# Half of the bias moved from VectorE to GpSimd, the scale of the levels folded into a mask, and the output scale one step later, in a fused convolution and 8-bit dense kernel

## The chip, the cores and the metric

The kernel runs on one core of a Trainium2 chip. The metric is the device time of one execution in microseconds (us), here the median of three runs. Engines are named as in the profile: PE is TensorE (PEld its weight loads), DVE is VectorE, ACT is ScalarE, POOL is GpSimd, SP is SyncE, which only issues DMAs in this kernel.

## The reference, cut to what matters

```python
def fake_quant(x, bits, axis):
    bound = 2 ** (bits - 1) - 1
    scale = max(abs(x), axis) / bound           # 1 where it is 0
    return round(clip(x / scale, -bound, bound)) * scale

h = conv1d(x, weight, taps=9, padding=4, groups=4)       # x: 64 x 64 x 1024
h = h + (cond_128 @ c_weight.T)[:, :, None] + fside_S_0[None, :, None]
xq = fake_quant(h, 8, axis=-1)                  # one scale per row of 1024
kq = fake_quant(ffn_kernel, 8, axis=0)          # 1024 x 1024, one scale per column
y = xq @ kq + fake_quant(ffn_bias, 16, axis=-1)
return x + fake_quant(y, 8, axis=-1)            # again one scale per row
```

## The kernel before, in words

The 4096 rows of length 1024 are cut into 32 tiles (`TILES`) of 128 rows: 8 samples by the 16 channels of one group. All five engines run program text written out by hand; each has its own loop over steps k, and semaphores join them. Several tiles are in flight at once. The order of the work is this order of the text, engine by engine; nothing is planned by a scheduler.

What happens to tile t, with the functions that do it:

- SP loads the convolution windows (`load_xwin`), and later the plain rows of x for the final sum (`load_x`, into a ring `o_sb` of 5, which also holds the output until `store` sends it).
- ACT rounds the windows to `x_hi` (`round_x`, L265), POOL makes the rest `x_lo` (`split`, L218), and PE does the convolution as 14 matmuls of 512 columns (`conv`, L386 and L396).
- DVE takes a maximum per block of the convolution (`column_max`, L564) and multiplies it by a 0/1 mask into `col_max` (L572). PE spreads it over the rows (`spread_max`, L407). DVE then makes the row maximum (L579), the scale of the levels `scale8` = maximum/127, not under 2^-126 (L582), the row's scale `row_scale` (L585), the inverse (L590) and half of the 8-bit levels (L594): all in `levels`. ACT makes the other half (`round_levels`, L304).
- PE transposes the levels one step later (`turn_levels`, L416), ACT copies them to `a_t` (`take_levels`, L295), and PE multiplies them by the dense kernel in two halves of 512 columns, 8 matmuls each (`dense`, L427): half 0 in step t+2, half 1 in step t+4 (`LAG = (2, 4)`). Each half has one PSUM bank of `dense_ps`.
- DVE scales each half in place in PSUM (`scale_half`, L550) and adds the bias `bq`, writing to the SBUF ring `y` of 5 tiles (`add_bias`, L559). The next `dense` of that half waits for `biased0` or `biased1`.
- One step behind the second half, in step t+5 (`TAIL = 5`), DVE takes the maximum of the whole row of y and makes its scale and inverse (`out_scale`, L604, L608, L611), ACT rounds y to levels and scales them back (`quantise`, L312 and L315), POOL adds x (`add_x`, L227), and SP stores.
- The last tile's output is made in halves by ACT (`quantise_last`, L323) and DVE (`add_x_last`, L618), and stored in halves (`store_last`, L185).

A write to a slot of `y` waits until the tile that had it five tiles before has been added (`o_made`). In a step k of its loop, DVE does: `column_max(k)`, `out_scale(k-5)`, `scale_half(k-2, 0)`, `levels(k)`, `add_bias(k-2, 0)`, `scale_half(k-4, 1)`, `add_bias(k-4, 1)`. ACT does: `take_levels(k-1)`, `round_x(k+2)`, `quantise(k-5)`, `round_levels(k)`. POOL does: `split(k+2)`, `add_x(k-5)`. PE does: `conv(k)`, `turn_levels(k-1)`, `dense(k-2, 0)`, `spread_max(k)`, `dense(k-4, 1)`; in step 32 the last transpose, of tile 31, stands behind `dense(30, 0)` and `dense(28, 1)`.

## Time and profile before

| | |
|---|---|
| median of 3 runs | 280.97 us (279.19 to 281.17) |
| the profiled execution | 278.56 us |
| its span, first to last instruction | 276.7 us |
| PE busy | 251.1 us, 91% of the span |
| DVE busy | 238.8 us, 86% |
| ACT busy | 185.2 us, 67% |
| POOL busy | 153.8 us, 56% |
| mean granted clock of PE | 0.986 |
| chain that ended last | PE 81%, DVE 8%, ACT 4%, DMA 3%, issue 2% |

The span is the stretch of one profiled execution that the trace shows; 1.86 us of that execution lie outside it. Instructions of one engine can overlap a little in the trace, so the start of the next one often lies before the end that the row gives. "Idle before" and the name behind the arrow say how long the engine stood still before a row and whose work released it. The chain that ended last is followed back from the last instruction, and what it names is what set the end.

### The profile page before, as it was taken

How to read it: one execution, taken by the hardware profiler on the slowest of the kernel's cores; microseconds unless marked ns; L12 is line 12 of the kernel's file. 1: busy time of each engine (PE TensorE's matmuls, PEld its weight loads, DVE VectorE, ACT ScalarE, POOL GpSimd, SP SyncE). 2: the span in 40 equal slices, each digit the busy share in tenths (PEclk: the TensorE clock that was granted, in tenths of full speed). 3: DMA queues.
4: the chain of work that ended last, by engine and by line, in shares of the span. 5: the costliest groups of instructions: out<-in, count | busy, mean ns of one | idle time of the engine just before them, and what ended most of it. 6: DMA issues, size and time to landing. Idle time of an engine off the chain costs nothing.

```text
span 276.7 us, 4240 instructions
## 1 busy us (share of the span) xinstructions
PE 251.1 (91%) x1372; PEld 163.5 (59%) x1372; DVE 238.8 (86%) x509; ACT 185.2 (67%) x278; POOL 153.8 (56%) x71
## 2 busy tenths in 40 slices
PE   7866769999999999999999999999999999997540
PEld 3555557666666666666666666666666666663210
DVE  1799964799999999999999999999999989999984
ACT  6257586477777777777777777777777767564762
POOL 2533333356666666666666666666666666533453
PEclk9979999999999999999999999999999999999996
DMA  6997322406666565566666766666666663333355
GB/s 253 416 408 301 123 84 103 153 0 227 223 203 212 211 202 212 203 217 217 209 204 210 230 228 228 228 227 226 219 203 197 218 218 117 144 142 139 107 220 219
DMA packets 15799, 56.04 MB, mean 203 GB/s; under 512 B 1954, under 2 KB 1954, under 8 KB 15778
## 3 DMA queue, kind: packets, MB, share of 16 engines
q1 hardware_dynamic: 15488, 55.71, 56.8%
q8 instruction: 11, 0.18, 0.3%
q10 hardware_dynamic: 290, 0.07, 0.1%
q14 instruction: 10, 0.08, 0.1%
HBM read 38.99 MB, written 16.78 MB: 202 GB/s over the span
## 4 chain that ended last, share of the span: by engine, by line
PE 81%; DVE 8%; ACT 4%; DMA 3%; issue 2%; SPq 0%; DVEq 0%
PE dense_ps L427 36%; PE conv_ps L396 31%; PE turn_ps L416 5%; PE conv_ps L386 5%; DMA k_raw<-ffn_kernel 3%; DVE dense_ps L550 2%; DVE y L559 2%; DVE y_max L604 2%; ACT kq L279 2%; PE small_ps L407 2%; PE dense_ps L449 1%; DVE k_max L523 1%; ACT a_int L304 1%; PE dense_ps L440 1%; ACT x_hi L265 1%
## 5 line engine op out<-in xcount | busy, mean ns | idle before, releaser
L427 PE MATMUL dense_ps<-kq,a_t 128*128 128x512 bf16 x512 | 120.6, 379 | 6.1 <-DVE y L559 5.0
L218 POOL TENSOR_TENSOR x_lo<-xwin,x_hi 128x1032 fp32r<-128x1032 f32 x32 | 76.6, 2393 | 80.8 <-ACT x_hi L265 80.8
L227 POOL TENSOR_TENSOR o_sb<-y,o_sb 128x1024 f32<-128x1024 f32 x31 | 73.9, 2384 | 32.8 <-ACT y L315 32.7
L427 PEld LDWEIGHTS dense_ps<-kq,a_t 128*128 128x128 bf16 x512 | 48.9, 101 | 53.7 <-issue 6.7
L295 ACT CAST a_t<-turn_ps 128x1024 bf16<-128x1024 int16 x32 | 32.4, 1012 | 48.5 <-PE turn_ps L416 48.5
L564 DVE TENSOR_REDUCE small_ps<-conv_ps 128x8 f32<-128x1024 f32 x32 | 39.4, 1232 | 13.8 <-PE conv_ps L396 13.5
L550 DVE SCALAR_TENSOR_TENSOR dense_ps<-dense_ps,row_scale,k_scale_b 128x512 f32<-128x512 f32 x64 | 47.7, 745 | 3.6 <-PE dense_ps L427 3.6
L312 ACT ACTIVATE y_int<-y,y_inv 128x1024 int16<-128x1024 f32 x31 | 35.6, 1148 | 22.3 <-DVE y_inv L611 22.1
L559 DVE TENSOR_TENSOR y<-dense_ps,bq 128x512 f32<-128x512 f32 x64 | 43.9, 685 | 2.8 <-ACT bq L288 1.6
L604 DVE TENSOR_REDUCE y_max<-y 128x1 f32<-128x1024 f32 x32 | 38.7, 1210 | 0.7 <-issue 0.2
L304 ACT ACTIVATE a_int<-conv_ps,inv 128x128 int16<-128x128 f32 x128 | 36.0, 363 | 1.1 <-DVE inv L590 1.1
L315 ACT ACTIVATE y<-y_int,y_scale 128x1024 f32<-128x1024 int16 x31 | 35.7, 1153 | 1.0
L396 PE MATMUL conv_ps<-x_hi,w_hi 128*128 128x512 f32 x128 | 36.2, 405 | 0.0
L265 ACT CAST x_hi<-xwin 128x1032 fp32r<-128x1032 f32 x32 | 33.8, 1055 | 3.0 <-DMA xwin<-x_windows 3.0
L396 PE MATMUL conv_ps<-x_hi,w_lo 128*128 128x512 f32 x128 | 35.5, 399 | 0.0
L396 PE MATMUL conv_ps<-x_lo,w_hi 128*128 128x512 f32 x128 | 35.2, 397 | 0.0
L396 PEld LDWEIGHTS conv_ps<-x_hi,w_lo 128*128 128x128 f32 x128 | 24.4, 191 | 6.2
L396 PEld LDWEIGHTS conv_ps<-x_lo,w_hi 128*128 128x128 f32 x128 | 24.0, 188 | 6.2 <-POOL x_lo L218 0.2
L396 PEld LDWEIGHTS conv_ps<-x_hi,w_hi 128*128 128x128 f32 x128 | 24.7, 193 | 4.8
L386 PE MATMUL conv_ps<-select,ctx 128*128 128x512 f32 x64 | 25.0, 474 | 1.9 <-ACT x_hi L265 1.6
L594 DVE TENSOR_TENSOR a_int<-conv_ps,inv 128x512 int16<-128x512 f32 x32 | 22.1, 691 | 1.1
L416 PE MATMUL turn_ps<-ident_b,a_int 128*128 128x128 bf16 x256 | 19.8, 220 | 1.6 <-ACT a_int L304 1.6
(55 smaller groups left out, 160.2 us busy)
## 6 DMA issues: line engine op xcount, KB each, us to landing
xwin<-x_windows SPq DMA_DIRECT2D x32, 516.0 KB, 4.8
o_sb<-x_rows SPq DMA_DIRECT2D x32, 512.0 KB, 5.3
out<-o_sb SPq DMA_DIRECT2D x31, 512.0 KB, 2.9
k_raw<-ffn_kernel SPq DMA_DIRECT2D x4, 1024.0 KB, 10.5
w_raw<-taps SPq DMA_DIRECT2D x2, 256.0 KB, 3.2
b_row<-ffn_bias SPq DMA_DIRECT2D x1, 512.0 KB, 15.9
out<-o_sb SPq DMA_DIRECT2D x2, 256.0 KB, 2.7
condt<-cond_t ACTq DMA_DIRECT2D x1, 32.0 KB
```

Source lines behind the costliest of these rows:

```text
L218: pool.tensor_tensor(x_lo[:, at].rearrange("p n b -> p (n b)"), xwin[:, t % XWIN, :], x_hi[:, at].bitcast(F32).rearrange("p n b -> p (n b) ...
L227: pool.tensor_tensor(o_sb[:, at, :], y[:, t % YRING, :], o_sb[:, at, :], ALU.add).then_inc(s["o_made"], 1)
L265: act.copy(x_hi[:, t % XSPLIT].rearrange("p n b -> p (n b)"), xwin[:, t % XWIN, :]).then_inc(s["hi_made"], 1)
L304: ins = act.activation(a_int[:, at, n * BLOCKS:(n + 1) * BLOCKS], conv_cols(at)[:, n, :], ACT.Copy, scale=inv8[:, at, n:n + 1])
L315: act.activation(y[:, t % YRING, :], y_int[:, t % 2], ACT.Copy, scale=y_scale[:, t % 2:t % 2 + 1]).then_inc(s["y_dequantised"], 1)
L386: mm = pe.matmul(conv_ps[:, at, hs, :].rearrange("p (n b) -> p n b", n=NH), ctx2[:, g].rearrange("k q o -> k (q o)"), select[:, ns].unsque ...
L396: mm = pe.matmul(conv_ps[:, at, hs, :].rearrange("p (n b) -> p n b", n=NH), w[:, ch, g].rearrange("p q o -> p (q o)"), x[:, x_at, hs * NH: ...
L427: mm = pe.matmul(dense_ps[:, h, :], a_t[:, t % LEVELS, q].rearrange("b j o -> b (j o)"), kq[:, q, half(h)], start=(q == 0), stop=(q == Q - 1))
L550: dve.scalar_tensor_tensor(out=dense_ps[:, h, :], in0=dense_ps[:, h, :], scalar=row_scale[:, t % RSRING:t % RSRING + 1], in1=k_scale_b[:, ...
L559: dve.tensor_tensor(y[:, t % YRING, half(h)], dense_ps[:, h, :], bq[:, half(h)], ALU.add).then_inc(s[f"biased{h}"], 1)
L564: dve.tensor_reduce(cmax_ps, conv_ps[:, t % 2].rearrange("p h (n b) -> p (h n) b", b=BLOCKS), AX_X, ALU.max, apply_absolute_value=True).th ...
L604: dve.tensor_reduce(y_max[:, at], y[:, t % YRING, :], AX_X, ALU.max, apply_absolute_value=True).then_inc(s["y_max_made"], 1)
```

## The change

Four things are changed:

1. The bias of half 1 is no longer added by DVE in the step from PSUM to SBUF. DVE's `scale_half(t, 1)` writes its product to `y` in SBUF, and POOL adds `bq` in place there (a new `add_bias` of POOL, one step later, in step t+5, at the head of POOL's step). For the last tile, 31, DVE does both halves as before. Half 0 is as before.
2. `dense(t, 1)` on PE waits for `scaled1` in place of `biased1`.
3. The factor 1/127 and the floor are put into the step that masks the column maximum (`mask_q` = mask/127, a scalar_tensor_tensor with maximum and multiply), so what is spread is already the scale. The operation that made `scale8` (L582) is gone; the inverse is taken from the row maximum itself. `mask_q` is made once at the start.
4. `TAIL` is 6, not 5: `out_scale`, `quantise`, `add_x`, the load of x for it and the store of a tile all stand one step later in their engines' loops.

```diff
-TAIL = LAG[1] + 1
+TAIL = LAG[1] + 2
...
+        def pool_adds(t, h):
+            return h == 1 and t < LAST
...
+            def add_bias(t, h):
+                wait(pool, f"scaled{h}", t + 1)
+                wait(pool, "b_made", 1)
+                pool.tensor_tensor(y[:, t % YRING, half(h)], y[:, t % YRING, half(h)],
+                                   bq[:, half(h)], ALU.add).then_inc(s[f"biased{h}"], 1)
...
             for k in range(TILES + TAIL):
+                if there(k - LAG[1] - 1) and pool_adds(k - LAG[1] - 1, 1):
+                    add_bias(k - LAG[1] - 1, 1)
                 if there(k + 2):
                     split(k + 2)
                 if 0 <= k - TAIL < LAST:
...
             def dense(t, h):
                 wait(pe, "a_made", t + 1)
-                wait(pe, f"biased{h}", t)
+                wait(pe, "scaled1" if h else "biased0", t)
...
             def scale_half(t, h):
                 wait(dve, f"dense_made{h}", t + 1)
-                dve.scalar_tensor_tensor(out=dense_ps[:, h, :], in0=dense_ps[:, h, :],
+                if pool_adds(t, h):
+                    wait(dve, "o_made", t - YRING + 1)
+                    to = y[:, t % YRING, half(h)]
+                else:
+                    to = dense_ps[:, h, :]
+                dve.scalar_tensor_tensor(out=to, in0=dense_ps[:, h, :],
...
-                dve.tensor_tensor(col_max[:, t % 2], cmax_ps.unsqueeze(2).to_broadcast([P, NS, Q]),
-                                  mask[:].unsqueeze(1).to_broadcast([P, NS, Q]), ALU.mult
-                                  ).then_inc(s["col_max_masked"], 1)
+                dve.scalar_tensor_tensor(out=col_max[:, t % 2],
+                                         in0=cmax_ps.unsqueeze(2).to_broadcast([P, NS, Q]),
+                                         scalar=127 * TINY,
+                                         in1=mask_q[:].unsqueeze(1).to_broadcast([P, NS, Q]),
+                                         op0=ALU.max, op1=ALU.mult
+                                         ).then_inc(s["col_max_masked"], 1)
...
-                dve.tensor_scalar(scale8[:, at], rmax_ps, 1.0 / 127, TINY, ALU.mult,
-                                  ALU.max).then_inc(s["scale_made"], 1)
+                dve.reciprocal(inv8[:, at], rmax_ps).then_inc(s["inv_made"], 1)
...
-                wait(dve, "scale_made", t + 1)
-                dve.reciprocal(inv8[:, at], scale8[:, at]).then_inc(s["inv_made"], 1)
...
                 wait(dve, "biased0", t + 1)
-                wait(dve, "biased1", t + 1)
+                if pool_adds(t, 1):
+                    wait(dve, "biased1", t + 1)
+                else:
+                    wait(dve, "biased_last", 1)
...
                     scale_half(k - LAG[1], 1)
-                    add_bias(k - LAG[1], 1)
+                    if not pool_adds(k - LAG[1], 1):
+                        add_bias(k - LAG[1], 1)
```

POOL's queue at the end of the program, before: the last `split`, then one `add_x` after another, of the tiles 24 to 30 (the number in `x_in` is the tile's, modulo 5).

```order
L218 TENSOR_TENSOR x_lo<-xwin,x_hi 128x1032 [waits conv_made,hi_made]
L227 TENSOR_TENSOR o_sb<-y,o_sb 128x1024 [waits x_in4,y_dequantised]
L227 TENSOR_TENSOR o_sb<-y,o_sb 128x1024 [waits x_in0,y_dequantised]
L227 TENSOR_TENSOR o_sb<-y,o_sb 128x1024 [waits x_in1,y_dequantised]
L227 TENSOR_TENSOR o_sb<-y,o_sb 128x1024 [waits x_in2,y_dequantised]
L227 TENSOR_TENSOR o_sb<-y,o_sb 128x1024 [waits x_in3,y_dequantised]
L227 TENSOR_TENSOR o_sb<-y,o_sb 128x1024 [waits x_in4,y_dequantised]
L227 TENSOR_TENSOR o_sb<-y,o_sb 128x1024 [waits x_in0,y_dequantised]
```

And now, from the `add_x` of tile 25 on. The rows that write `y` are the new `add_bias`, here of the tiles 27 to 30; the one of tile 28 stands behind the `add_x` of tile 26, the one of tile 30 behind that of tile 28.

```order
L236 TENSOR_TENSOR o_sb<-y,o_sb 128x1024 [waits x_in0,y_dequantised]
L229 TENSOR_TENSOR y<-y,bq 128x512 [waits b_made,scaled1]
L236 TENSOR_TENSOR o_sb<-y,o_sb 128x1024 [waits x_in1,y_dequantised]
L229 TENSOR_TENSOR y<-y,bq 128x512 [waits b_made,scaled1]
L236 TENSOR_TENSOR o_sb<-y,o_sb 128x1024 [waits x_in2,y_dequantised]
L229 TENSOR_TENSOR y<-y,bq 128x512 [waits b_made,scaled1]
L236 TENSOR_TENSOR o_sb<-y,o_sb 128x1024 [waits x_in3,y_dequantised]
L229 TENSOR_TENSOR y<-y,bq 128x512 [waits b_made,scaled1]
L236 TENSOR_TENSOR o_sb<-y,o_sb 128x1024 [waits x_in4,y_dequantised]
L236 TENSOR_TENSOR o_sb<-y,o_sb 128x1024 [waits x_in0,y_dequantised]
```

DVE's queue at the end, before: the output scale of tile 30 (L604, L608, L611), the second half of tile 31 (L550, L559), and the output scale of tile 31.

```order
L604 TENSOR_REDUCE y_max<-y 128x1 [waits biased1,biased0]
L608 TENSOR_SCALAR y_scale<-y_max 128x1 [waits y_dequantised,y_max_made]
L611 RECIPROCAL y_inv<-y_scale 128x1 [waits y_scale_made]
L550 SCALAR_TENSOR_TENSOR dense_ps<-dense_ps,row_scale,k_scale_b 128x512 [waits dense_made1]
L559 TENSOR_TENSOR y<-dense_ps,bq 128x512 [waits o_made,b_made,scaled1]
L604 TENSOR_REDUCE y_max<-y 128x1 [waits biased1,biased0]
L608 TENSOR_SCALAR y_scale<-y_max 128x1 [waits y_dequantised,y_max_made]
L611 RECIPROCAL y_inv<-y_scale 128x1 [waits y_scale_made]
```

And now: the second half of tile 31 stands ahead of the output scale of tile 30, and the two output scales follow one another (L569 is `scale_half`, L578 `add_bias`, L626, L630 and L633 are `out_scale`).

```order
L569 SCALAR_TENSOR_TENSOR dense_ps<-dense_ps,row_scale,k_scale_b 128x512 [waits dense_made1]
L578 TENSOR_TENSOR y<-dense_ps,bq 128x512 [waits o_made,b_made,scaled1]
L626 TENSOR_REDUCE y_max<-y 128x1 [waits biased1,biased0]
L630 TENSOR_SCALAR y_scale<-y_max 128x1 [waits y_dequantised,y_max_made]
L633 RECIPROCAL y_inv<-y_scale 128x1 [waits y_scale_made]
L626 TENSOR_REDUCE y_max<-y 128x1 [waits biased_last,biased0]
L630 TENSOR_SCALAR y_scale<-y_max 128x1 [waits y_dequantised,y_max_made]
L633 RECIPROCAL y_inv<-y_scale 128x1 [waits y_scale_made]
```

`out_scale(30)` waits for POOL's `biased1` there, and `out_scale(31)` is behind it.

## Rows read from the trace of the kernel before

**Rows 1.** Windows: one period of the main loop (busy us and instructions of each engine).

```profile
core 0: us, PE busy (x) PEld busy (x) DVE busy (x) ACT busy (x) POOL busy (x), PEclk, DMA share, GB/s
143.43:150.76 7.33, 7.33 (x41) 4.83 (x41) 6.73 (x15) 5.29 (x8) 4.76 (x3) 1.00 0.63 217
```

**Rows 2.** Chain that ended last, in order of time: start us, us, what.

```profile
48.20 0.46 PE turn_ps L416 x8
48.66 1.73 PE dense_ps L427 x8
...
52.72 2.82 PE conv_ps L396 x12
55.54 0.46 PE turn_ps L416 x8
...
246.31 1.24 DVE small_ps L564
```

**Rows 3.** Groups by line and shape: xcount | busy us, mean ns | idle before, releaser.

```profile
L227 POOL TENSOR_TENSOR o_sb<-y,o_sb 128x1024 f32<-128x1024 f32 x31 | 73.9, 2384 | 32.8 <-ACT y L315 32.7
...
L550 DVE SCALAR_TENSOR_TENSOR dense_ps<-dense_ps,row_scale,k_scale_b 128x512 f32<-128x512 f32 x64 | 47.7, 745 | 3.6 <-PE dense_ps L427 3.6
L559 DVE TENSOR_TENSOR y<-dense_ps,bq 128x512 f32<-128x512 f32 x64 | 43.9, 685 | 2.8 <-ACT bq L288 1.6
...
L315 ACT ACTIVATE y<-y_int,y_scale 128x1024 f32<-128x1024 int16 x31 | 35.7, 1153 | 1.0
L312 ACT ACTIVATE y_int<-y,y_inv 128x1024 int16<-128x1024 f32 x31 | 35.6, 1148 | 22.3 <-DVE y_inv L611 22.1
...
L572 DVE TENSOR_TENSOR col_max<-small_ps,mask 128x64 f32<-128x64 f32 x32 | 7.2, 224 | 1.1
...
L582 DVE TENSOR_SCALAR scale<-small_ps 128x8 f32<-128x8 f32 x32 | 5.3, 166 | 1.1
...
L210 POOL TENSOR_TENSOR w_lo<-w_raw,w_hi 128x512 fp32r<-128x512 f32 x2 | 2.7, 1352 | 4.3 <-ACT w_hi L258 4.3
```

**Rows 4.** Timeline, one step of the main loop: start us, us, engine, line [idle before].

```profile
144.90 0.22 DVE L572 TENSOR_TENSOR col_max<-small_ps,mask 128x64 f32<-128x64 f32 x1
...
145.40 0.41 PEld L407 LDWEIGHTS small_ps<-col_max,same_b 128*128 128x128 f32 x2
...
146.13 2.38 POOL L218 TENSOR_TENSOR x_lo<-xwin,x_hi 128x1032 fp32r<-128x1032 f32 x1 [2.02 <-ACT x_hi L265]
```

**Rows 5.** Timeline, behind the last convolution (tail).

```profile
256.10 1.01 ACT L295 CAST a_t<-turn_ps 128x1024 bf16<-128x1024 int16 x1 [3.39 <-PE turn_ps L416]
...
257.01 1.15 ACT L312 ACTIVATE y_int<-y,y_inv 128x1024 int16<-128x1024 f32 x1
...
258.19 1.15 ACT L315 ACTIVATE y<-y_int,y_scale 128x1024 f32<-128x1024 int16 x1
...
259.42 4.81 POOL L227 TENSOR_TENSOR o_sb<-y,o_sb 128x1024 f32<-128x1024 f32 x2 [5.30 <-ACT y L315]
...
262.42 1.22 DVE L604 TENSOR_REDUCE y_max<-y 128x1 f32<-128x1024 f32 x1
...
262.47 1.89 PE L427 MATMUL dense_ps<-kq,a_t 128*128 128x512 bf16 x8 [1.67 <-DVE y L559]
...
264.06 1.15 ACT L312 ACTIVATE y_int<-y,y_inv 128x1024 int16<-128x1024 f32 x1 [2.26 <-DVE y_inv L611]
```

**Rows 6.** Timeline, the end, and the one line L618.

```profile
270.02 2.35 POOL L227 TENSOR_TENSOR o_sb<-y,o_sb 128x1024 f32<-128x1024 f32 x1 [1.20 <-ACT y L315]
...
271.17 1.33 ACT L323 ACTIVATE y_int<-y,y_inv 128x512 int16<-128x512 f32 x2 [1.22 <-DVE y_inv L611]
...
272.39 0.33 SPq L180 DMA_DIRECT2D out<-o_sb  x1
...
273.61 0.36 SPq L185 DMA_DIRECT2D out<-o_sb  x1
...
L618 DVE SCALAR_TENSOR_TENSOR o_sb<-y_int,y_scale,o_sb x2: 739/831/923, 272.0 to 272.8; 128x512 f32<-128x512 int16 x2
```

More of the change, by code:

```diff
@@ L54, in build @@
         mask = sb("mask", [P, NS], F32)
+        mask_q = sb("mask_q", [P, NS], F32)
         same = sb("same", [P, CG], F32)
@@ L83, in build @@
         col_max = sb("col_max", [P, 2, NS, Q], F32)
-        scale8 = sb("scale8", [P, 2, NS], F32)
         inv8 = sb("inv8", [P, 2, NS], F32)
@@ L106, in build @@
             "cond_in", "b_in", "ones_made", "ident_made", "ident_b_made", "warm_made",
-            "mask_made", "same_made", "same_b_made", "select_made", "cond_made", "ctx_mm",
+            "mask_made", "mask_q_made", "same_made", "same_b_made", "select_made", "cond_made", "ctx_mm",
             "ctx_rounded", "ctx_made", "w_hi_made", "w_lo_made",
@@ L112, in build @@
             "hi_made", "lo_made", "conv_made", "col_max_made", "col_max_masked",
-            "max_spread", "row_max_made", "scale_made", "picked_made", "inv_made", "a_rounded", "a_rounded_dve", "a_turned",
-            "a_made", "dense_made0", "dense_made1", "scaled0", "scaled1", "biased0", "biased1",
+            "max_spread", "row_max_made", "picked_made", "inv_made", "a_rounded", "a_rounded_dve", "a_turned",
+            "a_made", "dense_made0", "dense_made1", "scaled0", "scaled1", "biased0", "biased1", "biased_last",
             "y_max_made", "y_scale_made", "y_inv_made", "y_rounded", "y_dequantised", "o_made", "last_rounded", "last_made")}
@@ L502, in _ @@
                               ).then_inc(s["same_made"], 1)
+            dve.wait_ge(s["mask_made"], 1)
+            dve.tensor_scalar(mask_q[:], mask[:], 1.0 / 127, None, ALU.mult
+                              ).then_inc(s["mask_q_made"], 1)
             dve.wait_ge(s["same_made"], 1)
@@ L559, in add_bias @@
                 dve.tensor_tensor(y[:, t % YRING, half(h)], dense_ps[:, h, :], bq[:, half(h)],
-                                  ALU.add).then_inc(s[f"biased{h}"], 1)
+                                  ALU.add).then_inc(s["biased_last" if h else "biased0"], 1)
             def column_max(t):
@@ L570, in column_max @@
                 if t == 0:
-                    dve.wait_ge(s["mask_made"], 1)
-                dve.tensor_tensor(col_max[:, t % 2], cmax_ps.unsqueeze(2).to_broadcast([P, NS, Q]),
-                                  mask[:].unsqueeze(1).to_broadcast([P, NS, Q]), ALU.mult
-                                  ).then_inc(s["col_max_masked"], 1)
+                    dve.wait_ge(s["mask_q_made"], 1)
+                dve.scalar_tensor_tensor(out=col_max[:, t % 2],
[4 more added lines that the diff above has]
+                                         ).then_inc(s["col_max_masked"], 1)
             def levels(t):
@@ L581, in levels @@
                 wait(dve, "row_max_made", t + 1)
-                dve.tensor_scalar(scale8[:, at], rmax_ps, 1.0 / 127, TINY, ALU.mult,
-                                  ALU.max).then_inc(s["scale_made"], 1)
+                dve.reciprocal(inv8[:, at], rmax_ps).then_inc(s["inv_made"], 1)
                 wait(dve, "scaled1", t - RSRING + 1)
                 dve.tensor_tensor_reduce(out=picked[:, at], in0=rmax_ps, in1=mask[:],
-                                         scale=1.0 / 127, scalar=0.0, op0=ALU.mult, op1=ALU.add,
+                                         scale=1.0, scalar=0.0, op0=ALU.mult, op1=ALU.add,
                                          accum_out=row_scale[:, r_at:r_at + 1]
                                          ).then_inc(s["picked_made"], 1)
-                wait(dve, "scale_made", t + 1)
-                dve.reciprocal(inv8[:, at], scale8[:, at]).then_inc(s["inv_made"], 1)
                 wait(dve, "inv_made", t + 1)
```

## Prediction

> **What bounds the kernel now.** I read the chain in order of time first, then one period by windows, then the timeline behind the last convolution.
>
> In the chain the first and the last step of a period of the main loop are transposes on PE, at 48.20 and 55.54 [rows 2]. What lies between is PE alone: transposes, dense matmuls, the convolution. It stays so until 246.31, where a DVE row takes the chain over [rows 2]. The window of one period shows PE busy 7.33 of 7.33 us at a granted clock of 1.00, DVE only 6.73, ACT 5.29, POOL 4.76 [rows 1]. So some 198 us (246.31 - 48.20, 27 periods) are PE's own pace, and an engine that gets lighter there gives nothing. What the change can move is the tail, 246.31 to 276.7, some 30 us in which no convolution is left and DVE, ACT and POOL finish the last tiles one behind the other.
>
> **The change part by part.**
>
> *Main loop, DVE.* Gone: one bias add of 685 ns and one L582 of 166 ns per step [rows 3]. DVE's load falls from 6.73 to about 5.9 us of 7.33. Cover was complete before, so this gives 0.
>
> *Main loop, the masked maximum.* It becomes a two-operation form. The trace has no such row at 64 elements. Bounds: 224 ns as now [rows 3], and 284 ns, since at 512 elements the two-operation form takes 745 against 685 ns [rows 3]; I take 0.25. It ends at 144.90 + 0.22 = 145.12 and PE's load that wants it stands at 145.40 [rows 4]. That is 0.28 us of cover against at most 0.06 lost: 0. Without the cover it would be 32 x 0.06 = 1.9 us. Starting the inverse without L582 brings `levels` forward by 0.17 us, hidden too. The one `mask_q` at the start stands long before the first convolution's maximum: 0.
>
> *Main loop, POOL.* Added: one add of 128x512 per step. No row shows it. From below, half of the 2384 ns for 1024 columns, 1.19; from above the strided 128x512 row, 1.35 [rows 3]. I take 1.24, nearer to the first, since both operands are contiguous there and here. POOL idles 2.02 us ahead of `x_lo` [rows 4] and the add is ready to go in just that gap (`scaled1` of the step before is older), so `x_lo` is not even late. POOL's load becomes 4.76 + 1.24 = 6.0 of 7.33. The sum is 0. With `TAIL` at 6, SP's loads and stores and ACT's rounding move by one step together and keep their distances; a write to `y` waits for an `add_x` one period nearer, with some 4 us still in hand in the loop.
>
> *Main loop, the SBUF port.* The rows show DVE's `scale_half` at 745 ns over all 64 instructions, whatever POOL did beside it [rows 3]. The Trainium skill (SBUF — State Buffer, Who interferes with whom) says that a DVE instruction with two SBUF inputs and a GpSimd instruction that reads SBUF shut each other out. By that rule nothing changes in the loop, since each of these DVE operations has its other input in PSUM.
>
> *The tail.* Here the order counts. POOL's queue now alternates: add of tile 27, `add_x(26)`, add of tile 28, `add_x(27)`, and so on. I follow it with the durations of the rows.
> - ACT takes the last levels at 256.10 to 257.11 [rows 5]. DVE's saved 0.17 us pulls this to 256.94 at best. In both kernels one `quantise` stands right behind: before that of tile 27, now that of tile 26. So one more tile than before is still to do.
> - `quantise(26)`: 2.33 us (257.01 to 259.34 [rows 5]), so 256.84 to 259.17. `add_x(26)`, 2.38 us and 0.08 later: 259.25 to 261.63. Only then the add of tile 28: 261.66 to 262.9. Its second half had been scaled by DVE some 6 us before.
> - `out_scale(28)` on DVE. From the start of L604 to ACT's start it takes 1.64 us (262.42 to 264.06 [rows 5]). DVE is just then busy with the first half of tile 31, which waits for `add_x(26)` because it has its slot of `y`, and with `scale_half(29, 1)` (0.69 + 0.75 from 261.7). So 263.2 to 264.8.
> - `quantise(28)` 264.8 to 267.15; `add_x(28)` 267.2 to 269.6; then, behind it, the add of tile 30: 269.6 to 270.85.
> - `out_scale(30)` 270.95 to 272.6. `quantise(30)` 272.6 to 274.9. Meanwhile `out_scale(31)` is done by 274.2, so the last rounding starts behind `quantise(30)` at 274.9, where before it started at 271.17 [rows 6].
> - `add_x(30)` 275.0 to 277.4, and the store of tile 30 is issued at 277.4. Before it was issued at 272.39, at once after the `add_x` that began at 270.02 [rows 6], and the span ended 276.7 - 272.39 = 4.3 us later, with 1 MB of stores in that time. The halves of the last tile are ready at 276.6 and 277.3 and queue behind that store on SP. So 277.4 + 4.3 = 281.7.
>
> The sum: 0 in the loop, 0 at the start (the chain is DMA, ACT and PE there, none of the edited lines), +5.0 in the tail. Against the profiled execution 278.56 + 5.0 = 283.6. That execution lies 2.4 us under the median of the runs shown, 280.97; on that median it is 286.0, which I give. Bounds of the sum: the new add at 1.19 or 1.35, twice on the chain, is -0.1 to +0.2; if the stores overlap fully, -0.4; the handoffs between engines that I took as 0.03 to 0.1 us are ten or so, +-0.5. That is +4.2 to +5.7, plus the runs' own scatter of about 1 us to either side.
>
> *The very end.* L618 took 923 ns the first time, while POOL was in `add_x(30)` until 272.37, and 739 ns the second time, with POOL idle [rows 6]. Now both fall wholly into `add_x(30)`. If the slowing stays at some 0.18 us each, they end at 277.6 and change nothing. The section of the Trainium skill named above lets the second comer wait for the whole of the first's instruction, since L618 reads `y_int` and `o_sb`, both in SBUF. By that, L618 would end at 277.4 + 1.5 = 278.9 and the span at 278.9 + 3.1 = 282.0, from the last store's 273.61 to 276.7 [rows 6]. The row bears it out only in part: 0.38 us of overlap cost 0.18.
>
> **The rivals.**
>
> *Not slower: DVE's queue decides the tail, not POOL's.* In the tail of before DVE sets most of the chain. If POOL kept pace, DVE would pay one more `out_scale`, +1.64, and save four bias adds of 685 ns and the 0.17: -2.9. That makes 281.0 - 1.3 = 279.7. It decides if the adds of tiles 28 and 30 find POOL free. Against it: the order has each of them behind an `add_x` that waits for ACT, and rows 5 put the first of these past 259.3. Chance 0.12, for a tail that overlaps better than I see, down to a small loss.
>
> *Faster: the main loop is DVE's after all.* Then 0.85 us x 27 = 23 us would go, to 258. Against it stands PE's 7.33 of 7.33 [rows 1]. A few tenths per step, through a handoff that the rows hide, are all I can imagine: 276. Chance 0.04.
>
> *Slower by more: the loop loses its cover.* If POOL's add took over 2.0 us, or the masked maximum over 0.5, each step would pay. 0.1 us a step is 3 us: 289. Nothing in rows 1 or 4 speaks for it. Chance 0.04.
>
> *Slower by more: PE's clock falls in the tail.* PE now stands still from about 260.6 to 263.2, where before a gap of 1.67 us was followed by 8 matmuls in 1.89 us [rows 5], so full speed. At the lower of the two levels `dense(30, 1)` and `dense(31, 1)` take some 3.8 us each. Then tile 31's half is ready only at 273.1 and holds `out_scale(30)` behind it, 2.2 us late: 288.2. Chance 0.08.
>
> **How the numbers follow.** The forecast has 0.72: 286.0, its own range 284.5 to 287.5. Its lower edge, the not-slower rival and the clock case give a range of 282.5 to 288.5 for 8 in 10. A measurement of this kernel tells about 1% (2.8 us) from no change. Slower by over 1%: 0.72 + 0.04 + 0.08, less 0.04 for a forecast that comes out short: 0.80. Within 1%: 0.12 + 0.04 = 0.16. Faster: 0.04.
>
> **What would show it.** In the changed trace the period should still be 7.33 us with PE full, DVE near 5.9 and POOL near 6.0. In the tail, the add of tile 28 should start the moment `add_x(26)` ends, near 261.7, and the add of tile 30 right behind `add_x(28)`, near 269.6; the chain there should run POOL, DVE, ACT, POOL, with POOL's share no longer nil. The last rounding should start near 274.9 and the last stores be issued near 278. I am wrong if POOL idles ahead of the adds of tiles 28 and 30, if the period differs from 7.33, or if the last rounding starts before 273.

## The result, and the profile after

The changed kernel takes 286.84 us (median of 4 runs, 286.26 to 287.83) against 280.08 us for the kernel before on the same chip. The ratio is 1.0244, with a 95% interval of 1.0185 to 1.0302: slower, though whether by less or more than 2% stays open. The medians are 6.8 us apart. The profiled execution took 286.26 us with a span of 284.5 us, 7.8 us more than the 276.7 us before.

Where the 7.8 us are is read from the starts of the column maximum (L564 before, L583 after) of three tiles. This is the one row that marks each step of the main loop.

| stretch | before | after | more |
|---|---|---|---|
| start to column maximum of tile 4 | 48.24 | 51.00 | +2.8 |
| from there to that of tile 31 | 198.07 | 198.30 | +0.2 |
| from there to the end (the tail) | 30.4 | 35.2 | +4.8 |

First, the main loop of the kernel after, one period by windows (to be laid beside [rows 1]), and the tail as one window:

```profile
core 0: us, PE busy (x) PEld busy (x) DVE busy (x) ACT busy (x) POOL busy (x), PEclk, DMA share, GB/s
146.28:153.63 7.35, 7.35 (x41) 4.83 (x41) 5.88 (x13) 5.30 (x8) 6.02 (x4) 1.00 0.65 216
249.30:284.50 35.20, 15.51 (x82) 6.91 (x79) 23.97 (x42) 17.84 (x20) 20.63 (x12) 0.86 0.50 180
```

PE is still busy in all of the period, 7.35 of 7.35 us. DVE has fallen from 6.73 to 5.88 us and POOL has risen from 4.76 to 6.02, each as worked out, and next to nothing of it shows in the time (+0.2 us over 27 periods). In the tail PE has nothing like a full load.

Whoever reads only the chain that ended last is led astray here. Part 4 of the page after says:

```profile
POOL 46%; issue 44%; DVE 3%; DMA 3%; ACT 1%; ACTq 0%; SPq 0%; POOLq 0%; DVEq 0%; PE 0%
```

The chain now runs through POOL and "issue" for most of the main loop, although the window above has PE full and the period is that of before. I read it as one way back among several that end close together. For what bounds the loop, the window and the period decide, and not the share.

Groups by line and shape, after; they answer to [rows 3]:

```profile
L229 POOL TENSOR_TENSOR y<-y,bq 128x512 f32<-128x512 f32 x31 | 39.3, 1267 | 1.0 <-DVE y L569 1.0
...
L569 DVE SCALAR_TENSOR_TENSOR y<-dense_ps,row_scale,k_scale_b 128x512 f32<-128x512 f32 x31 | 23.0, 743 | 0.8 <-POOL o_sb L236 0.6 <-PE dense_ps L438 0.2
...
L591 DVE SCALAR_TENSOR_TENSOR col_max<-small_ps,mask_q 128x64 f32<-128x64 f32 x32 | 7.2, 225 | 1.1
...
L604 DVE RECIPROCAL inv<-small_ps 128x8 f32<-128x8 f32 x32 | 6.7, 208 | 1.1
```

POOL's new add takes 1.267 us (1.24 taken, bounds 1.19 and 1.35). DVE's product into SBUF takes 743 ns, as into PSUM. The masked maximum with its second operation takes 225 ns where it was 224 [rows 3]. So the fusion of the scale costs nothing per instruction, and L582's 166 ns are gone.

The tail of the kernel after, timeline (to be laid beside [rows 5] and [rows 6]):

```profile
259.81 1.15 ACT L323 ACTIVATE y_int<-y,y_inv 128x1024 int16<-128x1024 f32 x1
...
262.22 2.35 POOL L236 TENSOR_TENSOR o_sb<-y,o_sb 128x1024 f32<-128x1024 f32 x1 [3.89 <-ACT y L326]
...
264.53 1.26 POOL L229 TENSOR_TENSOR y<-y,bq 128x512 f32<-128x512 f32 x1
...
264.70 0.69 DVE L578 TENSOR_TENSOR y<-dense_ps,bq 128x512 f32<-128x512 f32 x1 [2.03 <-POOL o_sb L236]
...
265.96 1.21 DVE L626 TENSOR_REDUCE y_max<-y 128x1 f32<-128x1024 f32 x1
...
266.19 1.89 PE L438 MATMUL dense_ps<-kq,a_t 128*128 128x512 bf16 x8 [2.60 <-DVE y L569]
...
272.31 1.26 POOL L229 TENSOR_TENSOR y<-y,bq 128x512 f32<-128x512 f32 x1
...
273.67 1.22 DVE L626 TENSOR_REDUCE y_max<-y 128x1 f32<-128x1024 f32 x1 [1.25 <-POOL y L229]
...
277.55 1.32 ACT L334 ACTIVATE y_int<-y,y_inv 128x512 int16<-128x512 f32 x2
277.72 2.34 POOL L236 TENSOR_TENSOR o_sb<-y,o_sb 128x1024 f32<-128x1024 f32 x1 [1.84 <-ACT y L326]
```

The add of tile 28 (264.53) follows `add_x(26)` (262.22) at once. DVE's L578, the first half of tile 31, has stood 2.03 us until that same `add_x(26)` was done. The output scale of tile 30 (273.67) stood 1.25 us for POOL's add of tile 30. The last rounding starts at 277.55.

### The profile page after: what moved, and what is told of

Same layout as the page of the kernel before. It is cut to its first block, busy times and chain, and to the rows that moved or that the text cites. A ratio compares the mean times of both kernels' runs of the same rounds, so it can differ in the third digit from the quotient of the medians.

```text
span 284.5 us, 4235 instructions
## 1 busy us (share of the span) xinstructions
PE 253.6 (89%) x1372; PEld 164.3 (58%) x1372; DVE 213.7 (75%) x447; ACT 185.0 (65%) x278; POOL 191.7 (67%) x102
## 4 chain that ended last, share of the span: by engine, by line
POOL 46%; issue 44%; DVE 3%; DMA 3%; ACT 1%; ACTq 0%; SPq 0%; POOLq 0%; DVEq 0%; PE 0%
POOL x_lo L221 26%; POOL y L229 14%; POOL o_sb L236 6%; DMA k_raw<-ffn_kernel 3%; DVE k_max L537 1%; DVE o_sb L640 1%; ACT kq L290 1%; ACTq L41 0%; DVE y_max L626 0%; ACT y_int L323 0%; ACT x_hi L276 0%; SPq L163 0%; DVE k_int L548 0%; DVEq L41 0%; PE dense_ps L460 0%
## 5 line engine op out<-in xcount | busy, mean ns | idle before, releaser
L438 PE MATMUL dense_ps<-kq,a_t 128*128 128x512 bf16 x512 | 122.3, 383 | 6.1 <-DVE y L569 3.5
L583 DVE TENSOR_REDUCE small_ps<-conv_ps 128x8 f32<-128x1024 f32 x32 | 39.4, 1232 | 41.2 <-PE conv_ps L407 41.2
L323 ACT ACTIVATE y_int<-y,y_inv 128x1024 int16<-128x1024 f32 x31 | 35.6, 1148 | 24.4 <-DVE y_inv L633 24.4
L626 DVE TENSOR_REDUCE y_max<-y 128x1 f32<-128x1024 f32 x32 | 38.7, 1210 | 2.0 <-POOL y L229 1.8
L229 POOL TENSOR_TENSOR y<-y,bq 128x512 f32<-128x512 f32 x31 | 39.3, 1267 | 1.0 <-DVE y L569 1.0
L407 PE MATMUL conv_ps<-x_hi,w_lo 128*128 128x512 f32 x128 | 36.2, 405 | 0.0
L276 ACT CAST x_hi<-xwin 128x1032 fp32r<-128x1032 f32 x32 | 33.8, 1056 | 3.2 <-DMA xwin<-x_windows 3.2
L569 DVE SCALAR_TENSOR_TENSOR dense_ps<-dense_ps,row_scale,k_scale_b 128x512 f32<-128x512 f32 x33 | 24.5, 743 | 6.4 <-PE dense_ps L438 6.4
L578 DVE TENSOR_TENSOR y<-dense_ps,bq 128x512 f32<-128x512 f32 x33 | 22.5, 682 | 3.9 <-POOL o_sb L236 2.0
L569 DVE SCALAR_TENSOR_TENSOR y<-dense_ps,row_scale,k_scale_b 128x512 f32<-128x512 f32 x31 | 23.0, 743 | 0.8 <-POOL o_sb L236 0.6
```

Source lines behind the costliest of these rows:

```text
L229: pool.tensor_tensor(y[:, t % YRING, half(h)], y[:, t % YRING, half(h)], bq[:, half(h)], ALU.add).then_inc(s[f"biased{h}"], 1)
L276: act.copy(x_hi[:, t % XSPLIT].rearrange("p n b -> p (n b)"), xwin[:, t % XWIN, :]).then_inc(s["hi_made"], 1)
L323: act.activation(y_int[:, t % 2], y[:, t % YRING, :], ACT.Copy, scale=y_inv[:, t % 2:t % 2 + 1]).then_inc(s["y_rounded"], 1)
L407: mm = pe.matmul(conv_ps[:, at, hs, :].rearrange("p (n b) -> p n b", n=NH), w[:, ch, g].rearrange("p q o -> p (q o)"), x[:, x_at, hs * NH: ...
L438: mm = pe.matmul(dense_ps[:, h, :], a_t[:, t % LEVELS, q].rearrange("b j o -> b (j o)"), kq[:, q, half(h)], start=(q == 0), stop=(q == Q - 1))
L569: dve.scalar_tensor_tensor(out=to, in0=dense_ps[:, h, :], scalar=row_scale[:, t % RSRING:t % RSRING + 1], in1=k_scale_b[:, half(h)], op0=A ...
```

## The experiments

Twelve runs, in the order in which they were made. "Tail" is from the start of the column maximum of tile 31 to the end of the span; before it is 30.4 us, after 35.2.

**1. The later step alone.** On the kernel before:

```diff
-TAIL = LAG[1] + 1
+TAIL = LAG[1] + 2
```

> The kernel before with TAIL = 6 and nothing else; VectorE still adds both biases. Theory 1 (the prediction's: the tail grows because GpSimd's adds of tiles 28 and 30 stand behind an add_x): here there are no such adds, so only one more output scale is left, about +1.6 us over before, a tail (from the last column maximum to the end) of about 32 us against 30.4. Theory 2 (the later step alone does it: one more quantise stands behind the last take_levels, the y slot of tile 31 is freed late, and the last rounding queues behind quantise(30)): the first half of tile 31 waits for add_x(26) until about 261.8 (times of the profile of before), the last rounding starts near 275.2 in place of 271.2, and the tail is 35 to 36 us, so +4.5 to +5.5 us. Theory 3, beside both: some 2 us of the changed kernel's loss are stretches at the lower TensorE clock in the start-up, and differ from run to run; then the runs of this kernel, whose start is that of before, show granted clocks between 0.96 and 0.99 too.

Measured: 288.77 us, ratio 1.0301 (1.0233 to 1.0368), tail 37.9 us. That is slower than the whole change. Theory 1's tail of 32 us is far off. Theory 2 holds in kind: the later step makes the tail grow by all that the change does, and more, without any add on POOL. Its size was too low, 37.9 us against a forecast of 35 to 36. Its tail has the row that matters, DVE's wait for the slot of `y`, and one that I had only as a rival, TensorE's clock:

```profile
265.13 0.69 DVE L559 TENSOR_TENSOR y<-dense_ps,bq 128x512 f32<-128x512 f32 x1 [2.04 <-POOL o_sb L227]
...
267.36 2.70 PE L427 MATMUL dense_ps<-kq,a_t 128*128 128x512 bf16 x8 [3.34 <-DVE y L559]
...
271.73 3.55 PE L427 MATMUL dense_ps<-kq,a_t 128*128 128x512 bf16 x8 [1.67 <-DVE y L559]
```

PE stands 3.34 us behind the waiting DVE. Of the two runs of 8 matmuls that follow the first takes 2.70 and the second 3.55 us, where 1.89 is normal [rows 5], so the lower of the two levels of the clock is on for the second. DVE waits for both. Together they are 2.5 us over the normal; 37.9 less that is 35.4 us, an estimate that is inside theory 2's range.

**2. VectorE adds in the tail.** The changed kernel, with VectorE's own bias add from tile 27 on:

```diff
         def pool_adds(t, h):
-            return h == 1 and t < LAST
+            return h == 1 and t < 27
...
                 wait(pe, "scaled1" if h else "biased0", t)
+                if h and t > 27:
+                    wait(pe, "biased_last", t - 27)
```

> The changed kernel, but VectorE adds the second half's bias from tile 27 on, as it did in the kernel before; GpSimd adds it for tiles 0 to 26 only, so no add stands behind an add_x in the tail. Theory 1: the tail comes back to about 32 us, some 3 us under the changed kernel. Theory 2: the tail stays at 34.5 to 36 us, within 1 us of the changed kernel and of the kernel with the later step alone.

Measured: 289.6 us, ratio 1.034 (1.0286 to 1.0395), tail 37.7 us. With no add behind an `add_x` in POOL's queue its tail is 2.5 us longer than that of the changed kernel, where theory 1 had it some 3 us shorter. Theory 1, the one of the prediction, falls here. Theory 2 had the tail within 1 us of both other kernels: it is so for experiment 1 and not for the changed one. Most of the 2.5 us is the clock again: the two runs of 8 matmuls take 2.53 and 3.57 us. PE stands 3.33 us ahead of them, for DVE's add of the bias; in the changed kernel it may use the bank once the half is scaled and stands 2.60 us, and the matmuls behind it are at full speed. That the shorter wait is what kept the clock up there is not shown.

**3. The add on POOL without the later step.** The changed kernel with `TAIL = LAG[1] + 1`.

> The changed kernel with TAIL back at 5. Theory A (a ring of waits): GpSimd's add, the output scale, the two quantise operations, add_x and the next add then follow one another in each period, 1.27 + 0.08 + 1.63 + 2.33 + 0.08 + 2.39 + 0.03 = 7.8 us against TensorE's 7.34, so the period becomes about 7.8 us and the time grows by about 0.46 x 27 = 12 us over the changed kernel's loop, less the 3 to 5 us that the shorter tail gives back: 292 to 297 us. Theory B (VectorE's 1.3 us of slack per period takes up the wait): the period stays 7.34 us and the tail is shorter, about 281 to 284 us.

Measured: 305.3 us, ratio 1.0897 (1.084 to 1.0954). The period is 7.75 us (windows; PE is busy 7.49 of it), so theory A. One of its steps:

```profile
252.79 1.27 POOL L229 TENSOR_TENSOR y<-y,bq 128x512 f32<-128x512 f32 x1
...
254.16 1.22 DVE L626 TENSOR_REDUCE y_max<-y 128x1 f32<-128x1024 f32 x1 [1.38 <-POOL y L229]
...
258.23 2.37 POOL L236 TENSOR_TENSOR o_sb<-y,o_sb 128x1024 f32<-128x1024 f32 x1 [4.16 <-ACT y L326]
...
260.55 1.27 POOL L229 TENSOR_TENSOR y<-y,bq 128x512 f32<-128x512 f32 x1
```

From one POOL add (252.79) to the next (260.55) it is 7.76 us, and the output scale waits 1.38 us for the add. The range of 292 to 297 was too low. The loop is 9.1 us longer than that of the changed kernel (207.4 against 198.3), less than the 12 expected. The tail is what I had wrong: I had let it get shorter, but the ring goes on in it, one tile per 7.7 us until the end, and it is 44.6 us. So in this kernel the add on POOL costs the loop its pace without the later step; the two parts of the change can't be judged apart.

**4. The last sum with one input in PSUM.** On the changed kernel:

```diff
-                    act.activation(y_int[:, at, half(h)], y[:, LAST % YRING, half(h)], ACT.Copy,
+                    act.activation(conv_ps[:, h, 0, :].bitcast(I32), y[:, LAST % YRING, half(h)], ACT.Copy,
...
-                    dve.scalar_tensor_tensor(out=o_sb[:, o_at, half(h)], in0=y_int[:, at, half(h)],
+                    dve.scalar_tensor_tensor(out=o_sb[:, o_at, half(h)], in0=conv_ps[:, h, 0, :].bitcast(I32),
```

> The changed kernel, but ScalarE writes the last tile's levels as int32 to two PSUM banks that are free by then, so VectorE's last two operations (L618 before, L640 after) have one input in SBUF and one in PSUM, and still overlap GpSimd's last add_x. Theory A (the two engines shut each other out of SBUF reads): the first of the two falls from 2.25 us to about 0.75 to 0.9, and is done before add_x(30); the last stores are then issued right behind that of tile 30, and the end comes 0.3 to 0.9 us earlier. Theory B (it was slow for another reason, the queue or the write to o_sb): it still takes over 2 us and the end stays.

Measured: 286.7 us, tail 35.3 us. The line of the changed kernel, and the same line here:

```profile
L640 DVE SCALAR_TENSOR_TENSOR o_sb<-y_int,y_scale,o_sb x2: 741/1496/2252, 278.4 to 280.5; 128x512 f32<-128x512 int16 x2
```

```profile
L642 DVE SCALAR_TENSOR_TENSOR o_sb<-conv_ps,y_scale,o_sb x2: 743/748/753, 278.7 to 279.4; 128x512 f32<-128x512 int32 x2
```

With both inputs in SBUF the first of the two takes 2252 ns and ends only behind `add_x(30)`; with one in PSUM (and as int32 in place of int16) they take 743 and 753 ns, beside the same `add_x(30)`. So theory A for the instruction. For the time it is worth nothing, and the 0.3 to 0.9 us expected did not come: from the start of `add_x(30)` to the end it is 6.8 us with it (277.72 to 284.5) and 6.9 without (278.14 to 285.0), since the store of tile 30 is issued only when that `add_x` is done, and all the last stores go with it.

**5 to 7. The start.** Five is the kernel before once more. Six and seven are the kernel before and the changed kernel with five idle fp32 matmuls of 512 columns, in three of TensorE's waits of the start-up:

```diff
+                if k == 1:
+                    keep_busy(conv_ps[:, 1, 0, :], 2)
                 if there(k):
                     conv(k)
...
                     spread_max(k)
+                    keep_busy(turn_bank, 1)
                     turn_levels(k - 1)
...
-                    k_turns(7, 8)
+                    k_turn(7)
+                    pe.wait_ge(s["a_made"], 2)
+                    keep_busy(turn_bank, 2)
+                    k_turn(8)
```

> The kernel before, unchanged, profiled once more. Theory L (the start-up part of the changed kernel's loss, 2.8 us in its profile, is a matter of when the lower TensorE clock falls in an execution, and the first profile of before was one with little of it): this profile shows two stretches at the lower clock in the first 50 us as the changed kernel's does, with the column maximum of tile 4 near 51 us in place of 48.2, and a span of 279 to 280 us. Theory C (the change brings them): the column maximum of tile 4 is near 48.2 us again, the clock near 0.986, the span 276.5 to 277.5 us.

Measured: 280.89 us (278.83 to 281.99), ratio 0.9999; column maximum of tile 4 at 48.98, clock 0.987. The profile alone spoke for theory C. The runs' clocks don't. Of 29 executions of the kernel before that were listed beside these kernels, 17 have a mean granted clock of 0.972 to 0.974 and take 281.3 to 282.4 us; 10 have 0.986 to 0.990 and take 277.9 to 279.5 us; two lie between. So before itself has two levels, some 2.8 us apart, and both of its profiles are of the quicker sort. All four runs of the changed kernel have 0.962 to 0.965.

The profiles of experiments 1 and 8 show it directly. Both are the kernel before with `TAIL` at 6, and experiment 8 with a larger ring of `y` (below); nothing else in the text of their start is changed. Their windows of the start, 14 to 24 and 40 to 48 us, first experiment 1, then 8 (the granted clock stands behind POOL):

```profile
14.00:24.00 10.00, 7.81 (x40) 5.93 (x36) 8.40 (x13) 5.48 (x6) 4.77 (x2) 0.66 0.98 402
40.00:48.00 8.00, 5.79 (x40) 3.41 (x38) 3.47 (x10) 4.44 (x9) 0.75 (x1) 0.79 0.38 133
```

```profile
14.00:24.00 10.00, 7.26 (x44) 5.55 (x42) 9.35 (x15) 6.34 (x7) 4.77 (x2) 0.83 0.95 387
40.00:48.00 8.00, 6.37 (x46) 4.94 (x46) 4.39 (x11) 6.07 (x12) 1.50 (x1) 1.00 0.38 133
```

The column maximum of tile 4 starts at 51.45 us in the first and at 48.91 in the second.

> The kernel before with five idle matmuls of 512 columns more on TensorE, in its three longest waits of the start-up (ahead of conv(1), ahead of the first turn_levels, between k_turn(7) and k_turn(8)). Under theory L these waits are what the clock falls after: with them filled the column maximum of tile 4 comes at 47 to 48.5 us in every execution, and the times lie at 277 to 279 us, closer together than the 279 to 282 us of before. Under theory C, or if the filling costs as much as it saves, the time stays at 279 to 281 us.

Measured: 279.02 us (277.9 to 279.49), ratio 0.992 (0.9879 to 0.9961): faster than before. All eight runs take what the quicker sort of before takes, so the slower sort is gone. The column maximum of tile 4 is at 48.65, just past the 47 to 48.5 expected.

> The changed kernel with the same five idle matmuls. What is left between it and the kernel before with them is the change without the start-up's clock: the prediction's tail term, +4.5 to +5.5 us. So near 283 us if the start-up is then free of the lower clock, and still near 287 us if the start-up's loss has another cause.

Measured: 284.07 us (283.26 to 285.41), ratio 1.0117 (1.0079 to 1.0156), tail 35.3 us. The windows of the start, 14 to 24 and 40 to 48 us, for before, after, and after with the waits filled:

```profile
14.00:24.00 10.00, 7.33 (x40) 5.83 (x41) 9.44 (x15) 6.43 (x7) 4.77 (x2) 0.83 0.97 380
40.00:48.00 8.00, 7.04 (x48) 5.31 (x48) 3.72 (x10) 5.41 (x10) 2.17 (x1) 1.00 0.39 135
```

```profile
14.00:24.00 10.00, 7.38 (x33) 5.60 (x32) 8.28 (x13) 5.55 (x7) 4.77 (x2) 0.66 0.99 397
40.00:48.00 8.00, 5.94 (x37) 3.68 (x38) 3.89 (x10) 4.44 (x9) 0.32 (x1) 0.79 0.37 133
```

```profile
14.00:24.00 10.00, 8.18 (x50) 5.48 (x47) 9.79 (x14) 6.52 (x7) 4.78 (x2) 1.00 0.99 395
40.00:48.00 8.00, 7.54 (x52) 5.48 (x52) 3.37 (x9) 5.21 (x9) 2.36 (x1) 1.00 0.37 135
```

The column behind POOL is the granted clock: 0.83 and 1.00, then 0.66 and 0.79, then 1.00 and 1.00. A mean of 0.66 over 10 us is 6.8 us at 1.2 GHz, a mean of 0.79 over 8 us is 3.4 us. In the second stretch the run of 8 dense matmuls (at 42.53 after, 41.42 before) takes 3.55 us in the changed kernel's profile in place of 1.89. With the starts filled in both, what is left between the two kernels is 284.07 - 279.02 = 5.05 us: the change itself, and close to the prediction's +5.0. It is not free of the clock altogether: three of the ten runs of experiment 7 still have 0.966 to 0.974. By the two profiles it is 4.5 us of span, +4.9 in the tail, +0.2 in the loop and -0.6 in the start.

**8. The ring of y.** The kernel of experiment 1 (the later step alone) with `YRING` 6 in place of 5.

> The kernel with the later step alone (TAIL = 6, VectorE adds both biases), with the ring of y at 6 tiles in place of 5. The tail of that kernel showed VectorE standing 2.04 us before the first half of tile 31, for add_x(26), and TensorE 3.3 us behind it, after which its clock fell. Theory R (the slot of y is what the later step costs): the wait is gone, TensorE does not stand so long, and the time falls from 288.8 us by 3 to 5 us, to 284 to 286 us. Theory O (one more output scale and quantise are the cost, the wait is hidden behind them): it falls by less than 1.5 us.

Measured: 284.81 us (282.07 to 286.2), ratio 1.0116 (1.0069 to 1.0163), tail 33.8 us against 37.9. Theory R: one slot more takes 4 us away. Two things are gone in this profile, the wait of 2.04 us for the slot and the lower clock in the tail, which had cost the two runs of 8 matmuls 2.5 us; PE stands half as long ahead of the first of them:

```profile
263.15 1.89 PE L427 MATMUL dense_ps<-kq,a_t 128*128 128x512 bf16 x8 [1.67 <-DVE y L559]
...
266.70 1.89 PE L427 MATMUL dense_ps<-kq,a_t 128*128 128x512 bf16 x8 [1.67 <-DVE y L559]
```

How the 4 us divide between the two is not shown. The runs have two sorts of clock here as well.

**9 and 10. A tail put together from this.** `TAIL` is 5 again and VectorE adds the second half's bias. The scale stays folded into the mask. POOL adds half 0 of the last three tiles, and the last second halves get banks and an order of their own (ten is nine with the idle matmuls):

```diff
         def pool_adds(t, h):
-            return h == 1 and t < LAST
+            return h == 0 and t >= TILES - 3
...
-                    mm = pe.matmul(dense_ps[:, h, :],
+                    mm = pe.matmul(conv_ps[:, 0, t % 2, :] if late_bank(t, h) else dense_ps[:, h, :],
...
                     turn_levels(k - 1)
+                    if k == TILES:
+                        dense(k - LAG[1] + 1, 1)
...
+                if k == TILES + 1:
+                    scale_half(k - LAG[1], 1)
+                    add_bias(k - LAG[1], 1)
+                    scale_half(k - LAG[0], 0)
+                    continue
```

> The kernel before (TAIL = 5, VectorE adds the second half's bias) with what the earlier runs say of the tail: the scale folded into the mask; GpSimd adds the bias of half 0 for tiles 29, 30 and 31, whose sums are wanted some 10 us later; dense(29, 1) stands ahead of dense(31, 0) on TensorE, the second halves of tiles 30 and 31 go to two banks of conv_ps that are free by then, and VectorE takes scale_half(29, 1) ahead of scale_half(31, 0). If VectorE's queue sets the tail of before, three bias adds (2.1 us) and the waits for the bank (about 1 us) go: the tail falls from 30.4 to 27 to 28.5 us and the time by 2 to 3.5 us, to a ratio of 0.988 to 0.993. If ScalarE and GpSimd's chain behind the last take_levels sets it too, it falls by under 1 us.

Measured: 279.1 us (276.69 to 280.44), ratio 0.9955 (0.9906 to 1.0004), tail 28.2 us. The tail fell by 2.2 us as expected. The time did not show it beyond its interval, and the ratio missed the 0.988 to 0.993 expected: this profile has a slow stretch in the start (column maximum of tile 4 at 50.79), and the start's clock scatters by more than the gain.

> The kernel with the rearranged tail and the five idle matmuls in the start-up. The two gains stand in different places and should add up: the filled start-up gave a ratio of 0.992 by itself, so 0.980 to 0.985, about 276 us, and a spread of under 2 us between the runs. If the tail's gain depends on the clock, less.

Measured: 276.82 us (276.57 to 277.13), ratio 0.9889 (0.9833 to 0.9946), tail 28.2 us. This beats both kernels: 2.6 us under the median of before beside it (279.45), 10 us under the changed one. The time is close to the 276 expected, and the gain over experiment 6 is 2.2 us, at the low end of 2 to 3.5. The ratio missed the expected 0.980 to 0.985, since the kernel before had a median of 279.45 beside this one and of 281.38 beside experiment 6. `dense(29, 1)` and `dense(31, 0)` still start only at 256.65, behind 1.37 us of waiting for DVE's bias of tile 28.

**11 and 12. Which queue in the changed kernel?** Both have the start filled. POOL does its adds ahead in the tail, and twelve has `YRING` 6 besides:

```diff
-                if there(k - LAG[1] - 1) and pool_adds(k - LAG[1] - 1, 1):
-                    add_bias(k - LAG[1] - 1, 1)
+                for t in range(k - LAG[1] - (k <= TILES), k - LAG[1] + (k >= TILES)):
+                    if there(t) and pool_adds(t, 1):
+                        add_bias(t, 1)
```

> The changed kernel with the start-up filled (284.07 us), and in the tail GpSimd does its adds ahead: tiles 27 and 28 before add_x(26), 29 before add_x(27), 30 before add_x(28). Theory Q (the prediction's: GpSimd's alternating queue is what sets the tail): the add of tile 28 ends near 256 us in place of 262, the add of tile 30 no longer holds out_scale(30), and the time falls by 3 us or more. Theory S (the slot of y: VectorE stands before the first half of tile 31 until add_x(26) is done, so out_scale(28) comes no earlier whatever GpSimd does): only the waits of out_scale(29) and out_scale(30) for the adds go, 0.56 and 1.25 us in the changed kernel's profile, and the time falls by 1 to 1.5 us.

Measured: 283.64 us (282.06 to 285.19), ratio 1.0107 (1.0067 to 1.0147), tail 35.6 us, against 284.07 for experiment 7. POOL's add of tile 28 now starts at 256.68 in place of behind `add_x(26)`. Theory Q falls, since the time does not drop by 3 us and DVE's wait for the slot is as long as before. The medians are only 0.4 us apart, short of theory S's 1 to 1.5, but the clocks differ: four runs here and six of experiment 7 have 0.983 or more, and their medians are 282.6 and 283.8 us, the 1.2 us of theory S. In this profile the low clock in the tail takes the gain back. Its rows:

```profile
256.68 1.27 POOL L229 TENSOR_TENSOR y<-y,bq 128x512 f32<-128x512 f32 x1 [0.95 <-DVE y L583]
...
262.09 0.69 DVE L592 TENSOR_TENSOR y<-dense_ps,bq 128x512 f32<-128x512 f32 x1 [2.03 <-POOL o_sb L236]
...
263.36 1.21 DVE L640 TENSOR_REDUCE y_max<-y 128x1 f32<-128x1024 f32 x1
...
263.59 3.57 PE L446 MATMUL dense_ps<-kq,a_t 128*128 128x512 bf16 x8 [2.60 <-DVE y L583]
```

> The same with the ring of y at 6 tiles. Theory Q: within 0.5 us of the kernel without the larger ring, since GpSimd's order was all. Theory S: the stand of 2.03 us before the first half of tile 31 goes as well, out_scale(28) and all behind it start about 2 us earlier, and the time is 1.5 to 2.5 us below that kernel, 280.5 to 281.5 us. Left over the kernel before with its start-up filled (279.02) is then the one step more of output scale and quantise, 1.5 to 2.5 us.

Measured: 280.6 us (279.81 to 281.35), ratio 0.9996 (0.9962 to 1.003), tail 32.2 us. The same places:

```profile
256.64 1.27 POOL L229 TENSOR_TENSOR y<-y,bq 128x512 f32<-128x512 f32 x1 [0.96 <-DVE y L583]
...
260.06 0.69 DVE L592 TENSOR_TENSOR y<-dense_ps,bq 128x512 f32<-128x512 f32 x1
...
261.66 1.21 DVE L640 TENSOR_REDUCE y_max<-y 128x1 f32<-128x1024 f32 x1
...
261.89 1.89 PE L446 MATMUL dense_ps<-kq,a_t 128*128 128x512 bf16 x8 [0.94 <-DVE y L583]
```

The first half of tile 31 starts at 260.06 in place of 262.09, with no wait, the output scale of tile 28 1.7 us earlier, and PE's run of 8 takes 1.89 in place of 3.57 us. Together 3.0 us, more than the 2.5 expected. The runs at a clock of 0.983 or more have medians of 282.6 us in experiment 11 and 280.5 here; at this like clock the slot is worth 2.1 us, close to the wait of 2.03, and the rest of the 3.0 goes with the clock. What is left over experiment 6 is 280.6 - 279.02 = 1.6 us, near the low end of the 1.5 to 2.5 expected. I take it for the one output scale and `quantise` more that the later step puts behind the last convolution; no run takes it away.

## Why the prediction came out as it did

The time was right: 286.0 forecast, 286.84 measured, inside 282.5 to 288.5. The mechanism was right in its rows and wrong in what it blamed, and the 286.0 was in part luck. It is 281.0 + 5.0; what was measured is 280.1 + 6.8. Of the 6.8 us some 5 are the change (experiments 6 and 7). I put the rest down to the clock of the start-up, for which the sum had no term.

*The main loop, 0.* Right but for 0.2 us over the 27 periods. The period stayed, with PE full, and DVE and POOL at 5.9 and 6.0 us as forecast. Of the two rivals in the loop neither came.

*The tail, +5.0.* Measured +4.8 in the profiles, and +4.9 between those of experiments 6 and 7. (Its bounds were added up wrongly: -0.1, -0.4 and -0.5 give +4.0 and not +4.2.) The steps can be compared one by one once the later start of the tail (249.30 against 246.31, 2.99 us) is taken off: the add of tile 28 at 261.5 (forecast 261.66), the add of tile 30 at 269.3 (269.6), the last rounding at 274.6 (274.9), the end at 281.5 (281.7). All four came within 0.4 us.

*The step that failed* is the sentence ahead of these: "Here the order counts. POOL's queue now alternates". POOL's queue does alternate, but it sets only the smaller part of what can be taken away. Without POOL's adds the later step costs no less (experiments 1 and 2: by the estimate above 35.4 us of tail without the low clock, and 35.2 in the changed kernel), with them done ahead it costs 0.4 us less by the medians and 1.2 at a like clock (11), and with a sixth slot of `y` 4 us go in one kernel and 3 in the other, a part of both through the clock (8 and 12). The prediction had the wait for the slot, as an aside with 0.3 us behind POOL's add. It is a second way to the same place: `out_scale(28)` is held at 263.2 by the slot and at 262.9 by POOL's add. Two waits that end 0.3 us apart look like one with a small extra. POOL's alone removed brought 0.4 us, both 3.5 (284.07 to 280.6); at a like clock it is 1.2 us and then 2.1 more. The slot's alone was removed only where POOL's adds were gone from the tail (8) or already ahead (12), so its worth in the changed kernel with nothing else changed is not shown.

*The not-slower rival* priced the case that POOL keeps pace at 279.7, 1.3 us under before. Experiment 11 frees POOL, and 12 the slot too, and the latter is still 1.6 us over its own base. I put the difference down to ScalarE's `quantise(30)`, which stands ahead of the last rounding; the forecast had it and this rival's price did not. No run separates it.

*The clock rival* named the right mechanism at the right gap. In the changed kernel's profile PE stood 2.60 us there (2.6 forecast) and the 8 matmuls behind took 1.89 us, so it did not come; in the profiles of experiments 1, 2 and 11 it did.

*The start, 0.* Not so in the profile: 2.8 us. The sum had no term for it. The changed kernel's profile has two stretches at 1.2 GHz where that of before has one. Experiment 1, whose start is that of before, has both stretches too, and experiment 8, with the same start, has one. About half of the executions of before are of the slower sort, and filling TensorE's waits takes the stretches away in the profiles of both kernels. So this is the scatter of the start-up's clock and not an effect that the edits are known to have. The four runs of before beside the result are two near 281 us and two near 279; all four of the changed kernel have a low mean clock (0.962 to 0.965), but one of experiment 4's had 0.977 and 283.81 us, with the same start. Whether the change makes it more frequent stays open. That run is near the 283.6 that the prediction worked out from the profiled execution of before. The 286.0 hit the median because it was the sum on the median of the runs, which lay 2.4 us higher; the reason for those 2.4 us was not asked, and by experiment 5's list it is this clock. That was the luck: two of the three runs behind that median lay near 281 us, where the slower sort lies, and all runs of the changed kernel are of that sort by their clock.

*The very end.* I took the slowing of L618 to stay at 0.18 us; the first of the two took 2.25, up to 0.55 us behind the end of `add_x(30)` (280.06). Experiment 4 shows that this comes of the input: with only its place and type changed the same instruction took 743 ns. That is the rule of the Trainium skill (SBUF — State Buffer, Who interferes with whom), that a DVE instruction with two inputs in SBUF and a GpSimd instruction that reads SBUF shut each other out. The trace agrees but for 0.2 us: alone the instruction takes 0.74 us, so it would have ended 0.74 us behind `add_x(30)`, and it ended 0.55 behind. In the span it cost nothing, so the rule's 282.0 was not needed either.

## What to carry to other kernels

In this loop, with the matmul engine full, the edits to the other engines cost 0.2 us and gained nothing, as long as no ring of waits grew longer than the period (experiment 3: 7.75 us against 7.34). The price stood where the loop ends. So a pipeline that gets one step deeper is to be followed tile by tile through the drain, that is the tail in which it runs empty, with every ring whose slots are freed one step later. When two waits end within a few tenths of a microsecond of each other, neither can be blamed from the trace: remove each, and both. And a kernel in which TensorE waits at the start, as this one does, should be compared by the granted clock of each execution, or with those waits filled, before a difference of 1% is put down to an edit.

## What had not been expected

- The start-up's clock: 17 of 29 executions of one and the same kernel at a mean of 0.972 to 0.974, 10 at 0.986 to 0.990, 2.8 us apart. Five idle matmuls in three waits gave a ratio of 0.992.
- All kernels with the scale folded into the mask need 198.3 us for the 27 periods between tiles 4 and 31 (after and its variants, but for experiment 3), all without it 198.07 or 198.08 (before, 1, 5, 6 and 8): 8 ns a step, in a loop where PE is full in both. The cause is not shown.
- A wait in the tail can bring a low clock, and the low clock the next wait: PE stood 3.3 us for DVE in experiments 1 and 2, its next matmuls took 2.5 to 3.6 us in place of 1.9, and DVE then waited for them. After 2.60 us the clock was low in experiment 11 and not in the changed kernel's profile nor in that of experiment 7.
